# Decoder layer on one core: gathered tokens turned by VectorE and spread by transfers, some copies moved to VectorE, and the final norm's chain interleaved

## The reference

```
x = layernorm(x + self_attention(x))       # 16 heads of 64, bias by relative distance
x = layernorm(x + cross_attention(x, ctx)) # 16 heads of 32, relative term, causal mask
x = layernorm(x + experts(x))

def experts(x):                            # E = 16 experts, K = 128 tokens each
    probs = softmax(x @ Wg + bg, axis=tokens)
    vals, idx = top_k(probs.T, 128)        # for each sequence and expert
    tok = x[idx]
    h = relu(tok @ w1[e] + b1[e]); h = relu(h @ w2[e] + b2[e]); h = h @ w3[e] + b3[e]
    return zeros.at[idx].add(h * vals)     # scatter-add over the experts
```

## Time and profile before

| | us |
|---|---|
| median of 3 runs (4250.17 to 4253.35) | 4250.72 |
| the profiled execution, its own time | 4248.04 |
| its span, first to last instruction | 4246.2 |

### The profile page before, as it was taken

The page is one execution under the profiler, slowest core; times in us unless marked ns, Lnnn a source line. Parts: engine busy times, 40 slices in busy tenths (PEclk is TensorE's granted clock), DMA queues, the critical chain, the costliest instruction groups (busy, mean ns, idle before and its releaser), DMA issues. The chain is left out here.

```text
span 4246.2 us, 91055 instructions
## 1 busy us (share of the span) xinstructions
PE 3872.7 (91%) x36924; PEld 2358.3 (56%) x36924; DVE 2466.8 (58%) x4776; ACT 1589.2 (37%) x3218; POOL 911.3 (21%) x1023
## 2 busy tenths in 40 slices
PE   5999998889999988899999888999998839999995
PEld 3676545556765456567754565667545614444442
DVE  3777435777774467777744677777436762222224
ACT  2444225744441357444413574444136710000002
POOL 2333100223331011233310112333101102222221
PEclk8999999999999999999999999999999969999998
DMA  8433259634332596343326963433278614454546
GB/s 252 114 98 98 90 192 345 213 119 113 93 93 90 226 326 209 107 113 93 93 90 246 322 213 91 115 93 88 90 275 310 196 66 115 122 118 128 118 129 208
DMA packets 286728, 659.65 MB, mean 155 GB/s; under 512 B 24529, under 2 KB 91137, under 8 KB 283089
## 3 DMA queue, kind: packets, MB, share of 16 engines
q1 hardware_dynamic: 270672, 616.41, 45.0%
q0 software_dynamic: 15344, 35.46, 4.6%
q10 hardware_dynamic: 320, 2.23, 0.2%
HBM read 385.17 MB, written 210.11 MB: 140 GB/s over the span
## 5 line engine op out<-in xcount | busy, mean ns | idle before, releaser
L506 ACT ACTIVATE sc<-sc,nmax 128x1024 f32<-128x1024 f32 x516 | 591.7, 1148 | 782.8 <-DVE nmax L732 782.1
L463 POOL TENSOR_SCALAR sc<-sc,pinv 128x1024 f32<-128x1024 f32 x516 | 578.8, 1122 | 1214.4 <-DVE pinv L740 1202.3
L1045 PE MATMUL psum<-pts,wct 32*64 32x256 f32 x8192 | 458.5, 376 | 3.5 <-issue 3.5
L1045 PE MATMUL psum<-xall,wct 32*64 32x256 f32 x8192 | 457.9, 376 | 0.0
L862 DVE CUSTOM_DVE_ANT_0 sc<-psum,big 128x896 f32<-128x896 f32 (+7 forms) x512 | 365.0, 754 | 146.1 <-PE psum L1238 130.5
L1030 PE MATMUL psum<-xt,w_all 128*128 128x256 f32 x1792 | 415.7, 385 | 22.9 <-PEq L1027 22.9
L757 DVE STREAM_TRANSPOSE pts<-sc 128x1024 f32<-128x1024 f32 (+3 forms) x342 | 333.7, 976 | 132.5 <-PE psum L1045 88.3
L1030 PEld LDWEIGHTS psum<-xt,w_all 128*128 128x128 f32 x1792 | 332.5, 190 | 127.7 <-issue 66.3
L506 ACT ACTIVATE sc<-sc,xmax 128x896 f32<-128x896 f32 (+7 forms) x512 | 394.1, 772 | 13.5 <-DVE xmax L862 10.7
L732 DVE CUSTOM_DVE_ANT_0 sc<-psum,table_a 128x1024 f32<-128x1024 f32 x258 | 312.2, 1210 | 111.9 <-PE psum L992 96.6
L1045 PEld LDWEIGHTS psum<-pts,wct 32*64 32x64 f32 x8192 | 308.1, 132 | 100.0 <-issue 49.3
(11 more groups left out here) (172 smaller groups left out, 5538.1 us busy)
## 6 DMA issues: line engine op xcount, KB each, us to landing
wct<-xall SPq DMA_DIRECT2D x576, 128.0 KB, 2.4
big<-skew_d SPq DMA_DIRECT2D x48, 1024.0 KB, 5.4
w_sb<-w_dram SPq DMA_DIRECT2D x48, 1024.0 KB, 5.4
big<-skew_d SPq DMA_DIRECT2D x48, 768.0 KB, 4.5
big<-skew_d SPq DMA_DIRECT2D x32, 896.0 KB, 4.6
big<-skew_d SPq DMA_DIRECT2D x32, 640.0 KB, 4.8
w_all<-wqkv_dram SPq DMA_DIRECT2D x33, 512.0 KB, 3.6
skew_d<-pts SPq DMA_DIRECT2D x8, 2048.0 KB, 6.9
```

The source lines that it names most:

```text
L463: pool.tensor_scalar(sc[k % 4][:, :], sc[k % 4][:, :], pinv[:, k % 4:k % 4 + 1], 1.0, ALU.mult, ALU.mult).then_inc(probs_scaled, 1)
L506: act.activation(tile, tile, ACT.Exp, bias=least, scale=-1.0, accum_out=total).then_inc(probs_ready, 1)
L1045: mm = pe.matmul(OSUM[HEAD[h], a, :], v_all[rows, ST * (b % GROUPS) + b // GROUPS, HEAD[h]], ptf[h][rows, QG * b:QG * b + QG], start=(b == ...
```

## The change

Three edits. In the diff stand, in this order, ACT's and DVE's part of the cross stream, ACT's and DVE's part of the experts, DVE's part of the final norm, and PE's layer 1.

1. **Tokens of the experts.** DVE transposes the 32x32 blocks of each sequence's gathered tokens into `tok_blocks`, one instruction of 128x512 for each sequence, and 16 transfers issued by ACT move the blocks to their partitions in `tokT`. The turning of expert e+1 stands in DVE's list behind the second hidden tile of layer 2 of expert e. PE's transposes and the four PSUM copies are gone. `tokT` now lies in another order, and layer 1 reads its 512 moving columns in 16 runs of 32.
2. **Second cross stream.** `copy_ot` goes from ACT to the head of DVE's step where unit u has four heads: three of 12 steps (positions 0, 2 and 3), and in the first group position 3 alone, 10 of 32 copies for each sequence and 40 of 128 in all.
3. **Final norm.** The seven small operations become five (`scale_step`), the last of which gives `fin_scale`; they stand behind the first five statistics of the next sequence. One small operation (`fhalf`) is added. ACT's list stays.

```diff
+        def ot_on_dve(u):
+
+            return u < NU and len(UNITS[u][2]) == HPQ
...
                 for u in range(NU + 4):
                     for v in range(XV):
-                        if LAST[v] + 3 == u:
+                        if LAST[v] + 3 == u and not ot_on_dve(u):
                             copy_ot(v)
...
+                def copy_ot(v):
+
+                    dve.wait_ge(ot_ready, v + 1)
+                    dve.tensor_copy(ot_sb[:, v % 2, :], OT).then_inc(ot_copied, 1)
                 for u in range(NU + 7):
+                    for v in range(XV):
+                        if LAST[v] + 3 == u and ot_on_dve(u):
+                            copy_ot(v)
...
+            def spread_tokens():
+
+                act.wait_ge(tok_turned, B)
+                act.sem_inc(tok_turned, -B)
+                act.sem_inc(tok_free, 1)
+                act.wait_ge(tokT_free, 1)
+                act.sem_inc(tokT_free, -1)
+                for g in range(GROUPS):
+                    for m in range(GROUPS):
+                        act.dma_start(tokT[DH * m:DH * m + DH, :, g, :, :], tok_blocks[DH * g:DH * g + DH, :, m, :, :]
+                                      ).then_inc(tokT_loaded, 16)
...
+            def turn_tokens(e):
+
+                for b in range(B):
+                    dve.wait_ge(gathered[b], 16 * (e + 1))
+                    dve.transpose(tok_blocks[:, :, :, b, :].rearrange("p c m i -> p (c m) i"),
+                                  tok[:, b, :].rearrange("p (j i) -> p j i", i=DH)).then_inc(tok_turned, 1)
...
+                        if layer == 1 and c == 1:
+                            dve.wait_ge(blocks_free, 1)
+                            dve.sem_inc(blocks_free, -1)
+                            turn_tokens(e + 1)
...
+            def scale_step(b, i):
+
+                ro, iv, mean = froot[:, b, :], finv[:, b, :], fmv[:, b, :, 0]
+                if i == 0:
+                    dve.wait_ge(fin_root, b + 1)
+                    dve.reciprocal(iv, ro).then_inc(fin_step, 1)
+                else:
+                    dve.wait_ge(fin_step, 4 * b + i)
...
             for b in range(B):
                 for t in range(ST):
                     if t % 4 == 0:
                         dve.wait_ge(fin_loaded[b][t // 4], 16)
+                    ins = dve.bn_stats(fstats[:, b, t, :], fin[b][:, t, :])
+                    if t == ST - 1:
+                        done(ins)
+                    if b > 0 and t < 5:
+                        scale_step(b - 1, t)
...
-                        if o == 0:
-                            pe.wait_ge((tok_by_act, tok_by_dve)[c % 2], c // 2 + 1)
+                        if o == 0 and c == 0:
+                            pe.wait_ge(tokT_loaded, 16 * GROUPS * GROUPS)
+                            pe.sem_inc(tokT_loaded, -16 * GROUPS * GROUPS)
+                            pe.sem_inc(blocks_free, 1)
+                        mm = pe.matmul(BANK[4 + o].rearrange("p (b g i) -> p b g i", b=B, g=GROUPS), w_e[0][:, c, P * o:P * o + P],
+                                       tokT[:, c, :, :, :].rearrange("p g b i -> p b g i"),
...
-                    if b == 1:
-                        turn_tokens(e + 1)
```

More of the change, by code:

```diff
@@ L1360, in decoder_layer @@
         we_free = [sem(f"w{n + 1}_free") for n in range(3)]
[L1361 to L1364, removed]
+        tok_turned = sem("tok_turned")
+        blocks_free = sem("blocks_free")
+        tokT_loaded = sem("tokT_loaded")
+        tokT_free = sem("tokT_free")
         hid_full = sem("hid_full")
@@ L1373, in decoder_layer @@
         fin_root = sem("fin_root")
+        fin_step = sem("fin_step")
         fin_scale = sem("fin_scale")
@@ L1462, in _ @@
                                ).then_inc(row_exp_ready, 1)
[L1463 to L1470, removed]
+            def spread_tokens():
[8 more added lines that the diff above has]
+                                      ).then_inc(tokT_loaded, 16)
+            act.sem_inc(tokT_free, 1)
+            spread_tokens()
             with act.Fori(0, E):
-                copy_tokens()
+                spread_tokens()
             def normalize(b):
@@ L1527, in _ @@
             NT = B * P
[L1529 to L1536, removed]
+            def turn_tokens(e):
[3 more added lines that the diff above has]
+                                  tok[:, b, :].rearrange("p (j i) -> p j i", i=DH)).then_inc(tok_turned, 1)
+            turn_tokens(0)
             with dve.Fori(0, E) as e:
@@ L1556, in _ @@
                 dve.sem_inc(y_full, -B)
+            def scale_step(b, i):
[5 more added lines that the diff above has]
+                    dve.wait_ge(fin_step, 4 * b + i)
+                if i == 1:
+                    dve.tensor_tensor(iv, iv, fhalf[:, b, :], ALU.mult).then_inc(fin_step, 1)
+                elif i == 2:
+                    dve.scalar_tensor_tensor(ro, ro, 0.5, iv, ALU.mult, ALU.add).then_inc(fin_step, 1)
+                elif i == 3:
+                    dve.reciprocal(iv, ro).then_inc(fin_step, 1)
+                elif i == 4:
+                    dve.scalar_tensor_tensor(fbias[:, b, :], mean, -1.0, iv, ALU.mult, ALU.mult).then_inc(fin_scale, 1)
             for b in range(B):
-                f = fin[b]
                 for t in range(ST):
@@ L1567, in _ @@
                 dve.tensor_scalar(fve[:, b, :], fmv[:, b, :, 1], EPS, None, ALU.add).then_inc(fin_var, 1)
[L1568 to L1581, removed]
+                dve.tensor_scalar(fhalf[:, b, :], fmv[:, b, :, 1], EPS, 0.5, ALU.add, ALU.mult)
+            for i in range(5):
+                scale_step(B - 1, i)
+            dve.wait_ge(fin_scale, B)
+            for t in range(ST):
+                if by_dve(B - 1, t):
+                    dve.tensor_scalar(fin[B - 1][:, t, :], fin[B - 1][:, t, :], fmv[:, B - 1, t, 0:1],
+                                      finv[:, B - 1, t:t + 1], ALU.subtract, ALU.mult).then_inc(fin_by_dve, 1)
         @block2.tensor
@@ L1591, in _ @@
             NT = B * P
[L1593 to L1602, removed]
             pe.sem_inc(y_taken, B)
@@ L1629, in _ @@
                             pe.wait_ge(hid_ready, c + 1)
+                            if c == DC - 1:
+                                pe.sem_inc(tokT_free, 1)
                         mm = pe.matmul(BANK[o][:, 0:NT], w_e[1][:, c, P * o:P * o + P], hid[0][:, c, :],
```

14 lines of the change are left out of this document (4 added, 10 removed).

## The result

The change is faster, as forecast, and by more than forecast: the medians lie 33.4 us apart, where 22.7 were forecast.

The account below looks back on a forecast made before the run. PE was taken to bound the experts, transfers and a DVE-ACT ring the final norm; in the cross stream PE waits for ACT. -26.2 - 0.3 + 11.0 + 2.8 - 10.0 = -22.7 from 4248.0 gave 4225.3, median 4228.0, range 4218 to 4244.

Parts of the forecast that it names:

- Tokens within the loop: Experts 0 to 14: removing PE's transposes saves 1.75 us each, 26.2 us in all, if the tokens arrive in time.
- the reserve: Expert loop: transferred tokens land at 37.4 us after the expert's start, PE wants them at 41.2, leaving 3.8 us.
- Rivals 1 and 2: Experts: tokens arrive late (4304 us, chance 0.08), or layer 1 reads slower (4283 us at 25%, chance 0.07).
- rival 1: Experts: ACT's issues cost over 0.90 us, so PE waits; loop loses from 1.02; 4304 us at 1.2, chance 0.08.
- Start: Tokens ahead of the loop, where nothing hides the path: +11.0 us, from 9.3 and 1.7, range +9 to +13.
- the clock term: First expert: 5.5 us of products at 1.2 GHz instead of about 2, losing 1.7 us.
- gain between 0 and 1.75: Last expert: its PE transposes, ahead of the outputs of sequences 2 and 3, also go; taken as 0.3 us gained.
- Final norm: Final norm: rounds of 9.1 us against 8.6, the end 2.8 us later, range 0 to +4.
- Ring: Final norm: ACT's root, normalize, root and DVE's chain wait for each other, giving rounds of 9.1 us.
- rival 4: Final norm: ACT's list does not hold the ring, the stores bind, 1.2 us gained; 4224 us, chance 0.10.
- Cross stream: Second cross stream: PE's waits before the turn at positions 0, 2 and 3 go, -10 us, range 0 to -14.
- Rival 3: Second cross stream: moving the copies gives nothing because DVE's maxima bound these steps; 4238 us, chance 0.15.

Follow-up runs that it names:

- the late turn: The changed kernel with DVE's four token transposes behind the fourth hidden tile of layer 2 instead of the second; 4315.65 us, ratio to before 1.0166.
- edit 1 alone: The kernel before with only the tokens turned by DVE and spread by transfers, cross stream and final norm as before; 4233.06 us, ratio 0.9969.
- edit 3 alone: The kernel before with only the final norm's small operations moved within the statistics of the next sequence; 4249.72 us, ratio 1.0001.

## Why the prediction was right, and where it was not

**Tokens within the loop: right.** 15 periods of 41.20 instead of 42.95 are the -26.2, and the reserve exists, 2.3 to 3.4 us instead of 3.8. The step with no row behind it, a read of 16 runs of 32 columns, costs nothing: the records of layer 1 follow each other every 0.43 us, as in before. This agrees with the Trainium skill ("SBUF — State Buffer", under Door 1), which says that consecutive accesses to the same 16-byte line go at full bandwidth. Rivals 1 and 2 are refuted here; the late turn, 6.9 us later, shows that rival 1 is real once the reserve is used up, and dearer than I had priced it.

**Start: the sum right, its parts off.** +10.3 for the path and +0.7 for the clock, against 9.3 and 1.7; that the sum comes out exactly is luck. The loss of the first expert's clock is 619.70 - 15 x 41.20 = 1.7 us after and 645.25 - 15 x 42.95 = 1.0 before. After PE had begun its products the low clock lasted 3.3 us and not 5.5. But it is not a fixed length that was misread. In the six other kernels with the same path it lasted 2.9 to 5.8 us, and the first expert was 1.5 to 2.95 us longer than the others (the late turn apart). Where PE turns the first expert's tokens (six kernels) it was 0 to 2.05 us longer. So one trace of before can't size the clock term; on average over these kernels it is +1.2 us.

**Last expert: wrong in sign.** -0.3 was +1.5 with edit 1 alone. The step that failed is "gain between 0 and 1.75": the loads of sequence 0 land later. At most a third of that comes of the scatters being closer to them; the rest is open.

**Final norm: mechanism right, size half.** Ring, waits and the delay of the first `fin_scale` (2.93 for 3.0) came as worked out, and rival 4 is refuted. Two sizes were too large. A statistic with a step beside it takes 0.67 us and not 0.71, so a round is 8.74 and not 9.1. The last chain takes 1.1 us and not 1.5, most likely since I had costed its steps by rows of a chain whose waits each also count their semaphore down; the two kinds of wait were not compared by themselves. Alone, the edit costs 1.4 us and not 2.8. In the whole change it costs less still, and so does the late load of sequence 0: there the first `fin_scale` comes 2.4 us later than before (55.95 from the last expert's start, 53.57 before), where the edit alone gives 2.9 and the tokens alone 1.5. Both hold back the same chain, which starts with the later of two: the root of sequence 0 or the first statistic of sequence 1, whose load lands last. That statistic starts 52.5 us after the last expert's start in after (4180.36 - 4127.87) and 53.0 with edit 3 alone (4211.67 - 4158.66), and the late root is hidden ahead of it. So +2.5 was forecast for the end, +1.4 and +1.5 came alone, and +0.9 together. One sign therefore failed: ACT's last stretch comes 28.3 us after its first root and not 31.4 (28.6 before), as the first root itself is 1.1 us late and the last stretch only 0.8. With edit 3 alone it is 30.0.

**Cross stream: the term that was mis-sized.** The waits named were removed: in one group the time from turn to turn fell from 8.06 to 7.68 (position 0), from 6.59 to 6.46 (position 2) and from 3.75 to 3.41 us (position 3), together 0.85, and 12 such groups make 10.2, the forecast's 10.3. Rival 3 is refuted. Part of it does return, as rival 3 would have it: at position 4 PE waits 0.38 longer for DVE's maximum, but 0.47 less for ACT's copy, so that step stays 4.85 us long. PE's waiting in the four streams is 9.9 us less. What I left out is the clock, which makes up most of the rest of the 16.6 us by which the streams are shorter. It acts in two places. Two stretches at 1.2 GHz less, at 1.6 us each, are 3.1. And the four starts, from first score to first turn, are 3.4 us shorter together: 0.6 are the waits of these first turns, which are at position 3 too, and the rest comes as in three of after's four streams the low clock of the start ended some 2 us earlier. How much this gives changes from kernel to kernel with the same streams: in five with after's the four starts take 44.5 to 47.0 us, and in five with before's 47.4 to 48.3. The stretches are 6 to 11 with the old streams and 4 or 5 with the new ones. Over these five executions each, the streams take 772.6 and 754.3 us on average, so the edit is worth some 18 us, of which the steps and the first turns explain 10.8. That the stretches follow from the wait at position 4 is borne out by the kernels that have it shorter still, and have none. The range allowed 14 for this term. The medians of before and after lie 33.4 apart and their profiles 28.9; the 4.5 between is of the size by which the streams of one code differ (769.1 to 777.5), though the other runs have no trace to show it.

**The range.** Its high end was added up 1 us too high (4238 + 2 + 1 is 4241), which changes nothing here.

## What to carry to other kernels

Price the turn of a tile by the engine that bounds at that place: the same 16 transposes are worth moving to a path many times as long inside the loop (14 us for 1.75), and cost 8 to 10 us ahead of it. Look at the granted clock behind PE's largest waits: there a wait cost more than its length, and taking the largest away gave back more than its length. When work is interleaved to hide a chain, look at what the engine on the other side has in its list between the two ends, and move that too: the same edit lost 1.4 us alone, and with the root moved as well the end came 3.3 us earlier than without both (86.76 for 90.06).

## What the runs showed that I had not expected

- A wait of 3.6 us ahead of a layer cost PE 2.95 us more, at a granted clock of 0.50 for 3.5 us and 0.74 for the next 4.2. Inside the cross streams there were 6 to 11 stretches of 3.4 us at 0.50 in the five kernels where PE waits 1.23 us ahead of the turn at position 4, four or five in the five where it waits 0.76, and none in the three where it waits 0.24.
- Transfers of 64 KB within SBUF, issued by ACT one after the other, land 2.1 us after their issue (2.0 to 3.5) in the last expert, which has no weight loads of SP beside them, and 4.2 us (2.0 to 5.9) in the expert shown above, which has, at the same 0.62 us an issue.
- A chain of five small DVE operations, each waiting for a counter that only rises, has them 0.22 us apart; seven whose waits also count the semaphore down stood 0.31 to 0.35 apart.
